# Attention and FFN megakernel: Q unpadded, scores on alternating halves of array rows, output in the transposes' PSUM bank

## The reference

```python
q = LN(x) @ (Wq + LoRA)                  # 16 heads of 64
k, v = ctx[:124] @ (Wk + LoRA), ctx[:124] @ (Wv + LoRA)
ki, vi = ctx[124:] @ Wk_ipa, ctx[124:] @ Wv_ipa       # 4 tokens of their own
o = softmax(q k^T / 8) v + softmax(q ki^T / 8) vi
x = x + o @ (Wo + LoRA) + bo
h = silu(conv1d(ternary(w1) @ quant8(LN(x))))         # 1024 channels, 3 taps
x = x + ternary(w2) @ quant8(h)
```

## Time and profile before

| what | value |
|---|---|
| three runs | 1680.71, 1683.01 (median), 1685.13 us |
| profiled execution, first to last instruction | 1677.3 us |
| PE busy | 88% |
| DVE busy | 78% |
| ACT busy | 71% |
| POOL busy | 44% |
| mean granted TensorE clock | 0.965 of full |

### The profile page before, as it was taken

The page is one execution under the profiler, slowest core; times in us unless marked ns, Lnnn a source line. Parts: engine busy times, 40 slices in busy tenths (PEclk is TensorE's granted clock), DMA queues, the critical chain, the costliest instruction groups (busy, mean ns, idle before and its releaser), DMA issues.

```text
span 1677.3 us, 33155 instructions
## 1 busy us (share of the span) xinstructions
PE 1469.8 (88%) x10540; PEld 1161.8 (69%) x10586; DVE 1310.7 (78%) x3159; ACT 1183.0 (71%) x3925; POOL 729.7 (44%) x1086
## 2 busy tenths in 40 slices
PE   6999998989899998989999998989999898998642
PEld 2578877777777777777777777777777777776521
DVE  5254698887879888887979888787988888787976
ACT  2277786968778696867778696877869686776621
POOL 0125444454444544453444444444454445444510
PEclk8699999999999999999999999999999999999955
DMA  6300100000010100000010000001010000000000
GB/s 186 116 28 15 29 15 28 15 26 27 13 39 13 40 13 27 14 26 27 13 40 13 28 13 26 27 13 39 13 40 13 27 13 26 27 1 27 1 13 13
DMA packets 41128, 47.13 MB, mean 28 GB/s; under 512 B 3008, under 2 KB 35200, under 8 KB 41088
## 3 DMA queue, kind: packets, MB, share of 16 engines
q1 hardware_dynamic: 41088, 46.62, 9.1%
HBM read 36.13 MB, written 10.49 MB: 28 GB/s over the span
## 4 chain that ended last, share of the span: by engine, by line
PE 34%; DVE 33%; ACT 20%; issue 12%; SPq 1%; DMA 0%; DVEq 0%; POOL 0%; ACTq 0%; POOLq 0%
ACT SM L647 8%; DVE GBS L872 7%; PE PS L467 6%; PE PS L429 4%; PE PS L445 4%; PE PS L524 4%; PE PS L410 4%; PE PS L454 3%; PE PS L480 3%; PE PS L419 3%; DVE GBS L883 2%; ACT H L672 2%; DVE GBS L862 2%; ACT GBS L677 2%; DVE H L890 2%
## 5 line engine op out<-in xcount | busy, mean ns | idle before, releaser
L1026 POOL TENSOR_TENSOR SM<-SM,RC 128x496 f32<-128x496 f32 (+1 forms) x512 | 337.0, 679 | 728.8 <-DVE RC L798 728.8
L647 ACT ACTIVATE SM<-PS,MX 128x124 f32<-128x124 f32 x1024 | 359.2, 365 | 199.3 <-DVE SM L804 196.1
L467 PE MATMUL PS<-KT,QM 128*128 128x128 f32 x2048 | 279.2, 279 | 26.4 <-ACT SM L647 26.3
L467 PEld LDWEIGHTS PS<-KT,QM 128*128 128x128 f32 x2048 | 249.3, 192 | 42.6 <-ACT SM L647 41.5
L1058 POOL TENSOR_TENSOR OTl<-OF,OTh 128x256 fp32r<-128x256 f32 x256 | 216.1, 844 | 5.6 <-ACT OF L641 5.6
L647 ACT ACTIVATION_READ_ACCUMULATOR SM<-PS,MX 128x1 f32 x1024 | 210.8, 206 | 0.0
L454 PE MATMUL PS<-IDF,SM 128*128 128x128 f32 x1024 | 168.5, 287 | 18.8 <-POOL SM L1026 18.8
L639 ACT ACTIVATE OTh<-PS 128x256 fp32r<-128x256 f32 x256 | 99.5, 389 | 101.8 <-PE PS L445 98.1
L802 DVE TENSOR_REDUCE MX<-PS 128x4 f32<-128x496 f32 x256 | 170.2, 665 | 0.0
L445 PE MATMUL PS<-PT,V 128*64 128x128 f32 x2048 | 168.8, 286 | 0.0
L445 PEld LDWEIGHTS PS<-PT,V 128*64 128x64 f32 x2048 | 106.8, 136 | 82.4 <-issue 75.5
(11 more groups left out here) (145 smaller groups left out, 3685.4 us busy)
## 6 DMA issues: line engine op xcount, KB each, us to landing
XIN<-in_x SPq DMA_DIRECT2D x16, 512.0 KB, 3.5
XRES<-in_x SPq DMA_DIRECT2D x16, 512.0 KB, 3.5
out_y<-H SPq DMA_DIRECT2D x16, 512.0 KB, 3.0
CRAW<-in_ctxT SPq DMA_DIRECT2D x16, 256.0 KB, 2.7
RRAW<-in_ctxT SPq DMA_DIRECT2D x32, 128.0 KB, 3.0
QM<-in_Wq SPq DMA_DIRECT2D x1, 1024.0 KB, 6.2
GBS<-in_Wo SPq DMA_DIRECT2D x1, 1024.0 KB, 12.9
k_ipa_columns<-H SPq DMA_DIRECT2D x1, 1024.0 KB, 5.2
```

What stands on the lines that cost most here:

```text
L467: m = mm(psS[:, h, :], QM[:, 2 * q + h // 2, h % 2, TOK * b:TOK * b + TOK], KT[:, 2 * q + h // 2, b, :], start=True, stop=True)
L647: m = act.activation(SM[s % 2][:, h, 0:ORG], psS[:, h, 0:ORG], ACT.Exp, bias=MX[s % 2][:, h:h + 1], accum_out=SU[s % 2][:, h:h + 1])
L1026: m = pool.tensor_tensor(part, part, RC[c % 2][:, 4 * i:4 * i + 4].unsqueeze(2).broadcast_to(shape), ALU.mult)
```

## The change

Three things change.

1. `QM` becomes `QT`, not padded, with half the size. A Q tile is copied by one ACT instruction of 128 partitions. For scores, the even head's matmul takes rows 0 to 63 of the array and the odd head's rows 64 to 127, in turns, and the two parities write to two banks (`psS` is now banks 0 and 1). POOL's zeroing of `QM` at the start goes; raw weights that were staged in `QM` move to `QT` and to a tile `STAGE`.
2. `psO` and `psT` are now in the same bank, 2. So PV waits that ACT has copied the transposes (`pt_done`, as before), and the transposes of a chunk wait for `ot_high` of the chunk before, a wait that PV had until now.
3. PV and the output copies move from the even half of step s+3 to the odd half of step s+2, each as the first thing of its half; POOL's low part and the output projection follow, one step earlier for a given chunk.

```diff
-        QM = sb("QM", [P, PAIRS, 2, T])
+        QT = sb("QT", [P, PAIRS, T])
+        STAGE = sb("STAGE", [P, 4096])
...
-        psS = PS[:, 0, :].rearrange("p (h k) -> p h k", h=4)
-        psT = PS[:, 1, :].rearrange("p (h k) -> p h k", h=4)
+        psS = PS[:, 0:2, 0:2 * TOK].rearrange("p r (a k) -> p r a k", a=2)
+        psT = PS[:, 2, :].rearrange("p (h k) -> p h k", h=4)
         psO = PS[:, 2, 0:2 * TOK].rearrange("p (a k) -> p a k", a=2)
...
             def p_v(g, s):
-                gc, c = chunk_at(g, s - 3)
+                gc, c = chunk_at(g, s - 2)
...
                     pe.wait_ge(pt_done, gc.count(CHUNKS, c + 1))
-                    need(pe, ot_high, gc.count(CHUNKS, c))
...
             def transpose_p(g, s):
                 gc, c = chunk_at(g, s - 2)
                 if gc.exists():
                     pe.wait_ge(p_done, gc.count(CHUNKS, c + 1))
+                    need(pe, ot_high, gc.count(CHUNKS, c))
...
                     for h in range(4):
-                        m = mm(psS[:, h, :], QM[:, 2 * q + h // 2, h % 2, TOK * b:TOK * b + TOK],
-                               KT[:, 2 * q + h // 2, b, :], start=True, stop=True)
+                        rows = slice(DH * (h % 2), DH * (h % 2) + DH)
+                        m = mm(psS[:, h % 2, h // 2, :], QT[rows, 2 * q + h // 2, TOK * b:TOK * b + TOK],
+                               KT[rows, 2 * q + h // 2, b, :], start=True, stop=True)
...
             def project_out(g, s):
-                gc, c = chunk_at(g, s - 4)
+                gc, c = chunk_at(g, s - 3)
...
                 if n % 2 == 0:
-                    p_v(g, n // 2)
                     transpose_p(g, n // 2)
                     scores(g, n // 2)
                     project_out(g, n // 2)
+                else:
+                    p_v(g, n // 2)
...
-                        act.activation(QM[0:64, 2 * q + a, 0, :], psU[u % 2][0:64, :], ACT.Identity)
-                        act.activation(QM[64:128, 2 * q + a, 1, :], psU[u % 2][64:128, :], ACT.Identity).then_inc(unit_free[u % 2], 1)
+                        act.activation(QT[:, 2 * q + a, :], psU[u % 2], ACT.Identity).then_inc(unit_free[u % 2], 1)
...
                 if n % 2 == 0:
+                    transposed_copy(g, n // 2)
+                else:
                     output_copies(g, n // 2)
-                    transposed_copy(g, n // 2)
```

More of the change, by code:

```diff
@@ L259, in program @@
         kipa_dram = nc.dram_tensor("k_ipa_columns", [GROUPS, P, PAIRS * NB * IPA], F32, kind="Internal").ap()
-        qm_flat = QM[:].rearrange("p a b t -> p (a b t)")
-        wq_raw = qm_flat[:, 0:2048].rearrange("p (k n) -> p k n", k=2)
-        wk_raw, wkr_raw, wv_raw, wvr_raw = (qm_flat[:, 2048 + 1024 * i:3072 + 1024 * i] for i in range(4))
-        q_up_t, k_up_t = (qm_flat[:, 6144 + 1024 * i:7168 + 1024 * i] for i in range(2))
+        wq_raw = STAGE[:, 0:2048].rearrange("p (k n) -> p k n", k=2)
+        q_up_t, k_up_t = (STAGE[:, 2048 + 1024 * i:3072 + 1024 * i] for i in range(2))
+        qt_flat = QT[:].rearrange("p a t -> p (a t)")
+        wk_raw, wkr_raw, wv_raw, wvr_raw = (qt_flat[:, 1024 * i:1024 * i + 1024] for i in range(4))
         kt_flat = KT[:].rearrange("p a b t -> p (a b t)")
@@ L445, in p_v @@
                         m = mm(psO[r:r + DH, h // 2, :], V[:, b, DH * (4 * q + h):DH * (4 * q + h) + DH],
[L446 removed]
+                               PT[:, 2 * (h % 2) + h // 2, :], start=True, stop=True)
                     m.then_inc(o_full, 1)
```

25 lines of the change are left out of this document (8 added, 17 removed).

## The result

| | before | changed |
|---|---|---|
| median of four runs | 1682.01 us (1680.71 to 1685.13) | 1756.52 us (1749.80 to 1759.94) |
| ratio | | 1.0431, 95% interval 1.0402 to 1.0460 |
| span of the profiled execution | 1677.3 us | 1747.7 us |
| mean granted clock | 0.965 | 0.938 |

What follows compares the result with a forecast made beforehand. It took no engine alone as the bound, but a chain over PE, DVE and ACT; +1.45 us a period over 14 periods gave +20, less 3 at the start: span 1694, median 1700 us, range 1655 to 1735.

Steps and rivals of the forecast that it cites:

- passage B: From F2, a feed-forward product on PE, to the maxima of step 4: PE is full and wins, -0.35 us a period.
- A: Second broadcast, steps 15 to 1: later scores, and output copies ahead of the broadcast's copy, +1.05 us a period.
- C: Exponentials of step 6 to those of step 7: longer loop through output copies and transposes, +0.65 us a period.
- F: Steps 13 to 14: output copies stand ahead of the last tanh, +0.55 us a period.
- D: First broadcast, from finished scores to the feed-forward product F1: 5.75 us in place of 4.48, +1.25 a period.
- E: From the feed-forward product F1 up to step 13: sooner scores and three Q copies less, -1.7 us a period.
- Start and end: Outside the full periods: -3 us before the loop from fewer Q copies, 0 for the first two periods and the tail.
- The price of the scores: Scores on PE: half rows pair, 0.73 us with changes of shape in place of 0.89, 0.16 less a step.
- rival 3: Scores on PE: rows don't pair, scores take 1.17 us, +4.8 a period, 1747 us; chance 0.12.
- The price on ACT: ACT's Q copies: one of two goes, some three of eight a period where ACT is full, 0.6 us each.
- The new edge: Transposes wait for output copies, scores stand behind: shortest way between exponentials 4.29 us in place of 3.62, 0.67 longer.
- Rival 1: Whole kernel: the gain comes through, A, C, D and F vanish, -2.8 us a period, 1641 us; chance 0.27.

Runs made afterwards that it cites:

- e4: The changed kernel with filler matmuls of 512 columns at two of PE's idle places, seven behind the K tile of half 30 and six behind PV in half 3: 1740.14 us.
- e13: The changed kernel with each Q tile copied by two ACT instructions of 64 partitions instead of one: 1797.34 us.
- e1: The kernel before with the shared bank and the moved PV and output copies, but Q still padded and copied twice: 1788.21 us.
- e10: The changed kernel with PV and output copies back in step s+3's even half, scores ahead of transposes, PT copy just ahead of exponentials: 1680.78 us.
- e11: e10 with ACT's PT copy right behind the output copies instead of just ahead of the exponentials: 1744.31 us.
- e12: e10 with POOL's low part ahead of its feed-forward product in half 1: 1725.22 us.
- e15: e12 with filler matmuls at PE's idle places, seven in half 2, five in half 9, three in half 10: 1682.03 us.
- e18: e15 with its seven filler matmuls moved from half 2 to half 4, between scores and transposes: 1680.95 us.
- e9: The changed kernel with heads sent in the order 0, 2, 1, 3, so that parities don't alternate: 1769.48 us, no ratio given.

## Why the prediction was wrong, step by step

The sign was right, and so was the mechanism as far as it was told: slower, by output copies ahead of both broadcasts' copies, by the longer loop from exponentials to exponentials, by the copies ahead of the last tanh. The range (1655 to 1735) did not hold the time; the 1700 were 56 too few. Two things failed: the walk through passage B, and the price of the waits on TensorE's clock, which stood at nothing. By the spans, 17 were expected and 70.4 came:

- **The sum of passages**, 1.45 us a period, measured 2.84. A, C, F and D with E are within 0.04 to 0.22 us of their terms; for D with E that is partly luck, since from the end of the scores to F1 it was +1.02 (5.50 against 4.48) where +1.25 stood, and the rest to step 13 -1.34 where -1.7 stood. The passage that failed is **B**: "then PE is full and wins 0.16 in the one step and ... 0.36 at the last". F2 was to be 0.2 late and was 0.45 late. Before, in period 3, the exponentials of step 1 start at 362.17, the transposes of that half at 363.24 and F2 at 367.20:

```profile
363.24 0.66 PE L454 MATMUL PS<-IDF,SM 128*128 128x128 f32 x4 [0.97 <-POOL SM L1026]
...
367.20 1.92 PE L524 MATMUL PS<-W,H 128*128 128x256 bf16 x16 [0.45 <-DVE H L890]
...
372.62 0.17 DVE L801 TENSOR_REDUCE MX<-PS 128x4 f32<-128x16 f32 x1 [1.86 <-PE PS L467]
```

In the changed kernel the same exponentials start at 374.08:

```profile
376.37 0.63 PE L454 MATMUL PS<-IDF,SM 128*128 128x128 f32 x4 [2.18 <-ACT OF L641]
...
379.56 1.92 PE L525 MATMUL PS<-W,H 128*128 128x256 bf16 x16
...
384.79 0.17 DVE L802 TENSOR_REDUCE MX<-PS 128x4 f32<-128x16 f32 x1 [2.12 <-PE PS L468]
```

The transposes are 2.29 behind the exponentials and not 1.07, and F2, which used to wait for DVE, now waits for PE. From F2 to the maxima PE wins 0.19 (5.23 against 5.42). Then 3 to 4 was 0.18 longer, not 0.36 shorter: the second F2 starts 0.18 later behind its exponentials, and its gain of 0.18 to the next scores ends in ACT's projection copies, which stand ahead of the exponentials of step 4. The prediction counted what PE saves as saved, in a stretch where DVE and ACT were only just hidden. (Its last line sizes such slips wrongly: six of 0.3 us are 1.8 us a period, not 4 a group, and 25 in 14 periods.)

- **The clock** was no term of the sum at all, and is the largest of what was missing: 1.6 us a period, 21 us over thirteen periods (e4 gives back 16). The prediction read the granted clock of the kernel before only to price a matmul. That new waits on PE would have a price beyond their length was nowhere asked. Thirteen of the 21 stretches lie behind the new waits of steps 1 and 4, eight behind the old one of step 15.
- **Start and end.** What was put at 0 for the first two periods was +7.3 us (74.1 and 87.5 us became 77.7 and 91.2): the change costs there as well, and one half-clock stretch lies there (197.4). The first exponentials come 1.2 us earlier, not 3. The last period with the tail costs 6.2, against 1.45 in the sum.

Together: 13 x 1.4 for the passages, 13 x 1.6 for the clock, 7.3 for the first two periods, 4.7 for the last and 1.8 for the start make 53 of the 53 us that were missing.

**The price of the scores.** Pairs came as forecast: x8 takes 0.72 (0.66 stood there), single starts at 909.472 and 909.479, 909.685 and 909.692, 909.797 and 909.804, 909.909 and 909.915, so 0.44 for all. The change of shape costs about 0.2 on the way in (the first pair is 0.21 from the second and not 0.11, and the scores start 0.09 late) and as much on the way out, where 0.14 each was taken: the scores occupy about 0.83, and not 0.73, of the 0.89 from before. Rows do pair, and rival 3 is out. As time on PE the saving is 0.06 a step, 1 us a period at best. As time to the result it is more: the last record of the scores ends about 0.25 earlier (0.09 + 0.72 against 1.06), and the three steps in which e13 gains on e1 gain 0.20 to 0.24 each. The Trainium skill's drain on a change of mode ("TensorEngine Tiling (Array Packing)", Tiling Modes) is there; of the 0.45 us that the halving gives to four short matmuls, the two changes take 0.39.

**The price on ACT.** Right in kind and nearly in size: 0.61 us for the one copy, and 2.08 us a period by the shortest steps of e13 and the changed kernel, so between three and four of the eight copies were on the path, where three stood. The rest of the 41 us between the two goes with nine fewer half-clock stretches.

**The new edge.** 4.48 against 4.29: 0.14 and not 0.04 from the copy's end to the transposes, and 1.27 and not 1.19 from there to finished scores. It cost what was said at 6 to 7, but not only there: PE waits in six places a period, not four, and behind the two longest (2.20 us until 876.28, 2.31 until 897.69) the clock falls in some periods.

**Rival 1** needed A + C + D + F under 2 us; they were 1.17 + 0.87 + 1.02 + 0.59 = 3.65. In e10, where the order is undone, the gain didn't come through either.

**What is open.** e10 differs from the changed kernel in the order on PE, the lag and ACT's order together, and e11 shows that they don't add up. Half rows without the shared bank can't be had here, since `psS` takes a second of eight banks that are all in use, so in this order the 30 us of e1 are part of the price of half rows. What decides in which period the clock falls behind an idle place stays open. Whether scores of both parities in one bank would do was not tried; the Trainium skill ("TensorEngine Tiling (Array Packing)", Restrictions and Gotchas) says that different row tiles can't use the same PSUM bank at a time. No run here shows it.

## What to carry to other kernels

Halving a matmul's array rows pays only if its saving exceeds two changes of shape, and only where PE is the chain; what it needs is priced first: here the shared bank alone cost 30 us in the order of the change, three times the 9 us that half rows win by the shortest steps. When an edit creates a wait on PE, price the wait and then look at what PE's clock does behind it, and count the half-clock stretches before a difference between two kernels is put down to the edit: fifteen filler matmuls a period took 43 us off one kernel here. And a passage in which an engine "wins" must be walked until the next engine's own work is met, because the neighbours are often only tenths of a us behind.

## What the runs showed of the hardware

- Behind idle places of about 2 us on PE the clock was halved for some us, up to three times in a period of 100 us. Filler matmuls took most of this away (e12 to e15: 26 stretches to 8, 1725 to 1682 us); such matmuls can be worth their time though nobody reads them.
- Whether the clock falls hangs on the place in time too: the same idle place was followed by half clock in every second or two of three periods, in a fixed cycle (e15, e18, the changed kernel); in the kernel before a wait of 2.20 us in every period was followed by it once in 14. Where one of two neighbouring places was filled, the clock fell at the other (e15, e18).
- Matmuls on the two halves of rows paired without alternating in program order (e9): eight records took 0.72 us in either order.
- A change between 128 and 64 rows costs about 0.2 us each way at the full clock beside matmuls of 0.11 us.
